# Context projections in blocks of three token tiles, keys in two arrays, keys of two head pairs loaded at once

## The chip, the cores and the metric

The kernel runs on one core of one Trainium2 chip. The metric is the device time of one execution in microseconds (us). Each of the core's engines works through its own list of instructions: TensorE (PE) for products and transpositions, VectorE (DVE), ScalarE (ACT) and GpSimd (POOL) for the rest, and SyncE (SP), which here only issues DMAs and waits. They are kept in step by semaphores. A DMA is carried out by up to 16 DMA engines of the core.

## What is computed

Four layers on x of 16 x 256 x 512, each added to x after a layer norm: a cross attention, a feed-forward layer with quantized weights, a second attention with a mask, and a feed-forward layer with LoRA experts. Only the first is touched. Cut to it:

```python
def _L0_xattn_ref(x, context, Wq, Wk, Wv, Wk_ip, Wv_ip, Wo, bo):   # 16 heads of 64
    ctx_txt = context[:, :77, :]                # 77 of the 256 context rows of a sample
    ctx_img = context[:, 77:, :]                # the other 179
    q = (x @ Wq)
    out = _attend(q, ctx_txt @ Wk, ctx_txt @ Wv)            # softmax(q k / 8) v for each head
    out_ip = _attend(q, ctx_img @ Wk_ip, ctx_img @ Wv_ip)
    return (out + out_ip) @ Wo + bo
x = x + _L0_xattn_ref(_layernorm(x), ctx_1024, ...)
```

All is float32. A product is made of three, with each operand split into a high and a low part (`product`, L189 to L195: high x high, high x low, low x high).

## The kernel before

**Two stages.** `cross_attention` calls `project_context` and then `attend_pairs`. The first makes keys and values of all 16 samples and writes them to DRAM (`k_d`, keys with a row for each of 1024 head dimensions and a column for each of 4096 context tokens; `v_d`, values with a row for each token). It also normalizes x, turns it and writes it (`xn_d`), and splits and turns the gate weights of the next layer (`wg_d`). The second reads all of that back, a pair of heads at a time.

**Blocks.** The text rows and the image rows of the samples have different weights, so `context_blocks` makes blocks of one kind: four of text, each the 77 rows of four samples (308 rows), then eight of image, each the 179 rows of two samples (358 rows). A block is cut into tiles of 128 rows. Where the last tile has fewer, it is loaded from `skip` rows further up, so that it still has 128; the repeated rows are not stored. Both kinds of block have three tiles.

**Jobs.** `jobs_of_block` gives eight key jobs (128 of the 1024 head dimensions for all rows of the block, 4 x 3 products with as many columns as the block has rows) and two value jobs for each tile (128 rows by 512 dimensions, 4 x 3 products with 512 columns). That is 14 jobs in a block, 168 in all. Job j uses the PSUM bank j % 6; ACT copies the result of even jobs to one of six stage slots, DVE of odd jobs (`job_out_of`, L528 and L479), and SP stores the slot (L421). A copy waits until the slot's store of six jobs before has landed (`stored`), and PE waits for the bank's copy of six jobs before (`job_out`).

**What is interleaved.** `turns` is a table of when PE transposes a tile: the next block's context tiles behind the jobs 1, 2 and 3 of a block, four tiles of x behind the jobs 5, 7, 9 and 11 of each image block, and gate weights in between. SP has one list: at job j it loads weight pieces, context rows (`load`, L363, one DMA for each run of rows of one sample within a tile), x rows (`load_x`, L368) and gate weights, then stores the turned tiles and the job's slot. A wait in this list holds up all that stands behind it. There is one buffer for context rows and one for x rows; a load waits until the last tile of the block before has been turned.

**The attention.** 128 steps, one for each sample and pair of heads. SP loads the keys of the pair five steps ahead (`load_k`, L680) into one of four buffers `kr`, in two DMAs of 64 rows, one for each head's half; ACT and POOL split them three and two steps ahead (`keys_high`, L922; `keys_low`, L762). Every second step SP loads values, and in every step it waits for the queries that DVE has finished and stacks them with four DMAs (L695). ACT must see a stack landed before it overwrites its source two steps on (`queries_high`, L953).

Of the kernel before, what the change touches and what calls it, by code (L numbers as in the profile page):

```python
# [16 lines left out]
F32 = mybir.dt.float32  # L17
# [6 lines left out]
P = 128  # L24
B, S, D = 16, 256, 512
TOK = B * S
CT = 512
NCH = TOK // CT
# [5 lines left out]
HEADS, DH = 16, 64  # L34
INNER = HEADS * DH
TEXT = 77
# [159 lines left out]


IMG = S - TEXT
TB, IB = 4, 2


class Rows:
# [16 lines left out]


def context_blocks():
    blocks = []
    for g in range(B // TB):
        blocks.append(Rows("text", g * TB, TB * TEXT, [((g * TB + i) * S, TEXT) for i in range(TB)]))
    for g in range(B // IB):
        blocks.append(Rows("img", g * IB, IB * IMG, [((g * IB + i) * S + TEXT, IMG) for i in range(IB)]))
    return blocks


# [4 lines left out]

def cross_attention(nc, a, x_in, ctx_in, x1, xt_d, wg_d, wq, first_x, big, scal, ident, neghalf):
    xn_d = nc.dram_tensor("xn_parts", (B, P, 2, KD, S), F32R).ap()
    k_d = nc.dram_tensor("k_rows", (INNER, TOK), F32).ap()
    v_d = nc.dram_tensor("v_rows", (TOK, INNER), F32).ap()
    with Phase(nc, "xo", leaf=False) as top:
        wo = top.sb("Wo", [P, 2, NPAIR * D], F32R)  # L240
        project_context(nc, a, x_in, ctx_in, xn_d, k_d, v_d, wg_d, wq, wo, ident, neghalf)
        attend_pairs(nc, a, x_in, xn_d, k_d, v_d, x1, xt_d, wq, wo, first_x, big, scal, ident, neghalf)


def project_context(nc, a, x_in, ctx_in, xn_d, k_d, v_d, wg_d, first, second, ident, neghalf):


    blocks = context_blocks()
    NBLK, NTX = len(blocks), B // TB
    jobs = [(c, job) for c, block in enumerate(blocks) for job in jobs_of_block(block)]  # L250
    first_job = [next(i for i, (c, _) in enumerate(jobs) if c == b) for b in range(NBLK)] + [len(jobs)]
    NJ = len(jobs)
# [30 lines left out]
    with Phase(nc, "pr") as ph:  # L283
        w = [first, second, ph.sb("w2", [P, 2, KD * INNER], F32R), ph.sb("w3", [P, 2, KD * INNER], F32R)]
        raw = ph.sb("raw", [P, NRAW, INNER])
        rows = ph.sb("rows", [P, MOST, D])
# [4 lines left out]
        NQ = D // QB  # L291
# [22 lines left out]
        def stores(j):  # L314

            c, job = jobs[j]
            block = blocks[c]
            slot = stage[:, j % NST]
            if job[0] == "k":
                each = TEXT if block.kind == "text" else IMG  # L320
                off, nb = (0 if block.kind == "text" else TEXT), block.n // each
                cols = slice(block.first * S, (block.first + nb) * S)
                return [(k_d[job[1] * P:(job[1] + 1) * P, cols].rearrange("p (b n) -> p b n", n=S)[:, :, off:off + each],
                         slot[:, 0:block.n].rearrange("p (b n) -> p b n", n=each))]
            lo, count, skip = block.tiles[job[1]]
            cols = slice(job[2] * CT, (job[2] + 1) * CT)
            return [(v_d[row:row + length, cols], slot[skip + at:skip + at + length, :]) for at, row, length in block.pieces(lo, count)]
# [28 lines left out]
        with nc.Block() as block_:  # L356
            @block_.sync
            def _(sp):
# [43 lines left out]
                for j in range(NJ):  # L402
                    c = jobs[j][0]
                    for at in range(0 if j == 0 else j + 2, j + 3):
                        for i in piece_at.get(at, []):
                            load_piece(i)
                    if c + 2 < NBLK and j == first_job[c] + len(blocks[c + 1].tiles):
                        load(c + 2)
                    if j == first_job[NTX - 1]:
                        load_x(0)  # L410
                    for i in range(KF):
                        if j == first_job[WFIRST + i // WPER - 1] + WAT[i % WPER] + 1:
                            load_gate(i)
                    if c >= NTX and c + 1 < NBLK and j == first_job[c] + 12:
                        load_x(c - NTX + 1)
                    for n, kind, _, _ in turns_at.get(j - 1, []):
                        if kind != "c":
                            store_aside(n)
                    sp.wait_ge(job_out[j % 2], j // 2 + 1)
                    for dst, src in stores(j):  # L420
                        sp.dma_start(dst, src).then_inc(stored[j % NST], 16)  # L421
# [168 lines left out]
def attend_pairs(nc, a, x_in, xn_d, k_d, v_d, x1, xt_d, wq, wo, first_x, big, scal, ident, neghalf):  # L590
# [13 lines left out]
    with Phase(nc, "at") as ph:  # L604
# [35 lines left out]
            ph.sem(n) for n in ("row_max", "all_max", "settled", "spacer_d", "spacer_p", "spacer_a"))  # L640
        cleared, bo_ready, bo_high, bo_low = (ph.sem(n) for n in ("cleared", "bo_ready", "bo_high", "bo_low"))
        x_ready, v_ready = ([ph.sem(f"{n}{i}") for i in range(2)] for n in ("x_ready", "v_ready"))
        q_ready, k_ready = [ph.sem(f"q_ready{i}") for i in range(NQ)], [ph.sem(f"k_ready{i}") for i in range(NKR)]
        res_ready, stored = ([ph.sem(f"{n}{i}") for i in range(NY)] for n in ("res_ready", "stored"))
        s_full, max_done, exp_done, sum_done, rec_done, norm_done, v_high, v_placed, k_high, k_low = (
            ph.sem(n) for n in ("s_full", "max_done", "exp_done", "sum_done", "rec_done", "norm_done", "v_high", "v_placed", "k_high", "k_low"))
# [18 lines left out]
        with nc.Block() as block:  # L665
            @block.sync
            def _(sp):
# [5 lines left out]

                def load_k(n):
                    b, h = n // NPAIR, 2 * (n % NPAIR)
                    cols = slice(b * S, (b + 1) * S)
                    if n >= NKR:
                        sp.wait_ge(k_low, n - NKR + 1)
                    for rows in (0, 64):
                        sp.dma_start(kr[rows:rows + 64, n % NKR], k_d[h * DH:(h + 2) * DH, cols].rearrange("(h r) n -> r h n", r=DH)  # L680
                                     ).then_inc(k_ready[n % NKR], 16)

                def load_v(g):
                    b, p = g // (NPAIR // 2), g % (NPAIR // 2)
# [28 lines left out]
                load_x(0)  # L713
                load_k(0)
                load_v(0)
                for n in range(1, LEAD_K - LEAD_Q + 1):
                    load_k(n)
                sp.wait_ge(cleared, 1)
                for row in (0, 32):
                    sp.dma_start(xn[row:row + 1, :], a["L0_xattn_bo"].rearrange("(o n) -> o n", o=1)).then_inc(bo_ready, 16)  # L720
                load_x(1)
                for s in range(FIRST, LAST + 2):
                    if FIRST < s and s + LEAD_K < N:
                        load_k(s + LEAD_K)
                    if 0 < s + 1 < N and s % 2:
                        load_v((s + 1) // 2)
                    if 0 <= s < N and s % NPAIR == 0:
                        load_res(s // NPAIR)
                    if s >= 0 and (s + 10) % NPAIR == 0 and 2 <= (s + 10) // NPAIR < B:
                        load_x((s + 10) // NPAIR)  # L730
                    if s + LEAD_Q < N:
                        stack_q(s + LEAD_Q)
                    done = s - LAG_O - NPAIR - 2
                    if done >= 0 and done % NPAIR == 0:
                        store(done // NPAIR)
                    if out_tile(s - 4):
                        store_turned(*out_tile(s - 4))
                    if s == N:
                        sp.wait_ge(q_full, N)
                        for i in range(2):  # L740
                            sp.wait_ge(xt_stored[i], 16 * NB * NTE // 2)
                        sp.dma_start(wq[:, 0, 0:KD * CT].bitcast(F32), xt_d[0]).then_inc(first_x, 16)
# [147 lines left out]
            def _(act):  # L890
# [25 lines left out]
                    ins.then_inc(exp_done, 1)  # L916

                def keys_high(n):
                    act.wait_ge(k_ready[n % NKR], 32 * (n // NKR + 1))
                    if n >= NK:  # L920
                        act.wait_ge(s_full, n - NK + 1)
                    act.activation(ks[:, n % NK, :, 0, :], kr[:, n % NKR], ACT.Copy).then_inc(k_high, 1)  # L922
# [1974 lines left out]
```

## Time and profile before

| | us |
|---|---|
| median of three runs (3362.14 to 3363.12) | 3362.61 |
| the profiled execution | 3366.48 |
| its span, first to last instruction | 3364.4 |
| PE busy in the span | 3144.0 (93%) |
| DVE, ACT, POOL busy | 1965.9, 1665.2, 792.3 |
| context projection, from the first to the last product of it | 22 to 445 |
| first attention | 456 to about 1240 |

The profile has one execution. A line of a timeline gives the start, the length, the engine (SPq and the like are an engine's issuing of DMAs), the line of the code, the operation, output<-input, and how many instructions are merged; in brackets the idle time before it and what ended it. Matmuls are pipelined, so the pace of a row of products is read from their starts and not from their lengths. The share of the DMA engines is a mean over 16.

### The profile page before, as it was taken

The page shows a single profiled execution, that of the slowest core. Times are in us where ns is not written, and L with a number is a line of the kernel's source. Part 1 is how long each engine was busy: PE and PEld are TensorE (multiplying, and loading weights), DVE is VectorE, ACT ScalarE, POOL GpSimd, SP SyncE. Part 2 cuts the span into 40 slices and gives each one's busy share as a digit, 9 for nine tenths or more (in the row PEclk, how much of TensorE's full clock was granted, in tenths as well). Part 3 has the DMA queues.
Part 4 walks back from the last instruction along what each step waited for, and adds up shares of the span by engine and source line. Part 5 has one row for each costly group of instructions (what it writes and reads, how often), then busy time and mean ns, then how long its engine had stood idle before and what let it go on. Part 6 is the DMA issues. An engine that isn't in the chain of part 4 may idle for free. (4 is left out here: it accounts for less than half of the span.)

```text
span 3364.4 us, 51211 instructions
## 1 busy us (share of the span) xinstructions
PE 3144.0 (93%) x16792; PEld 2687.5 (80%) x16792; DVE 1965.9 (58%) x3425; ACT 1665.2 (49%) x3210; POOL 792.3 (24%) x882
## 2 busy tenths in 40 slices
PE   7999979999999979999996798996979999999998
PEld 6988969999999957887874576885857888888886
DVE  3245549999999965557888995554843222222211
ACT  3132249999999953336676786564722111111110
POOL 0000038888888830000000200003700000000000
PEclk9999989999999999999998898998989999999999
DMA  6487755555555545556666676444831110001000
GB/s 187 120 250 228 228 171 165 172 177 173 171 167 173 158 154 195 180 172 204 225 217 220 215 261 224 156 162 158 265 116 60 38 38 27 24 26 38 32 26 13
DMA packets 370165, 503.46 MB, mean 150 GB/s; under 512 B 58940, under 2 KB 237420, under 8 KB 366032
## 3 DMA queue, kind: packets, MB, share of 16 engines
q1 hardware_dynamic: 356458, 473.37, 45.0%
q0 software_dynamic: 4768, 18.88, 1.6%
q10 hardware_dynamic: 8720, 8.41, 0.7%
q8 instruction: 124, 2.03, 0.2%
q14 instruction: 95, 0.78, 0.1%
HBM read 292.86 MB, written 174.11 MB: 139 GB/s over the span
## 5 line engine op out<-in xcount | busy, mean ns | idle before, releaser
L2625 DVE SCALAR_TENSOR_TENSOR lf_hT<-lf_hb,lf_hT 128x512 fp32r<-128x512 f32 x128 | 88.5, 691 | 571.0 <-ACT lf_hT L2701 571.0
L2701 ACT ACTIVATE lf_hT<-lf_hb 128x512 fp32r<-128x512 f32 x128 | 76.6, 598 | 669.1 <-PE lf_py L195 639.6
L775 POOL TENSOR_TENSOR at_prob<-at_prob,at_rec 128x308 f32<-128x308 f32 (+1 forms) x256 | 261.3, 1043 | 85.5 <-DVE at_rec L815 85.2
L915 ACT ACTIVATE at_prob<-at_sc,at_nm 128x77 f32<-128x77 f32 (+1 forms) x1024 | 277.8, 386 | 6.9 <-DVE at_nm L802 4.5
L193 PE MATMUL lf_hb<-lf_xT,lf_w 128*128 128x512 f32 x512 | 204.8, 400 | 1.3 <-DVE lf_hT L2625 1.3
L195 PE MATMUL lf_hb<-lf_xT,lf_w 128*128 128x512 f32 x512 | 203.7, 398 | 0.0
L195 PE MATMUL lf_py<-lf_w,lf_hT 128*128 128x512 f32 x512 | 203.7, 398 | 0.0
L193 PE MATMUL lf_py<-lf_w,lf_hT 128*128 128x512 f32 x512 | 203.4, 397 | 0.0
L194 PE MATMUL lf_hb<-lf_xT,lf_w 128*128 128x512 f32 x512 | 203.3, 397 | 0.0
L194 PE MATMUL lf_py<-lf_w,lf_hT 128*128 128x512 f32 x512 | 203.2, 397 | 0.0
L808 DVE TENSOR_REDUCE at_sums<-at_prob 128x4 f32<-128x308 f32 (+1 forms) x256 | 166.1, 676 | 17.3 <-ACT at_prob L915 17.1
L2554 POOL TENSOR_SCALAR lf_var<-lf_mv 128x1 f32<-128x1 f32 x32 | 7.3, 229 | 716.4 <-DVE lf_mv L2577 716.4
L193 PE MATMUL at_qb<-at_xT,xo_Wq 128*128 128x256 f32 x512 | 150.0, 293 | 23.5 <-DVE at_qst L832 12.3
L762 POOL TENSOR_TENSOR at_ks<-at_kr,at_ks 128x512 fp32r<-128x512 f32 x128 | 165.4, 1292 | 13.0 <-ACT at_ks L922 13.0
L193 PE MATMUL dn_py<-qf_wd,dn_om 128*128 128x512 f32 x384 | 150.7, 393 | 15.9 <-DVE dn_om L1969 15.9
L802 DVE TENSOR_REDUCE at_nm<-at_sc 128x4 f32<-128x308 f32 (+1 forms) x256 | 159.6, 665 | 5.9 <-PE at_sc L991 5.9
L193 PE MATMUL pg_bank<-qu_xs,qg_wg 128*128 128x512 f32 x384 | 153.6, 400 | 8.7 <-DMA qg_wg<-gate_parts 8.7
L819 DVE TENSOR_TENSOR at_pT<-at_tp,at_pT 128x1024 fp32r<-128x1024 f32 x128 | 156.4, 1222 | 3.4 <-ACT at_pT L928 0.3
L193 PE MATMUL pu_bank<-qu_xs,qu_wu 128*128 128x512 f32 x384 | 150.6, 392 | 7.6 <-SPq L1298 5.7
L1014 PE MATMUL at_sc<-at_pT,at_vs 128*128 128x256 f32 x1024 | 153.1, 292 | 1.4 <-issue 1.4
L194 PE MATMUL pg_bank<-qu_xs,qg_wg 128*128 128x512 f32 x384 | 151.1, 394 | 0.0
L195 PE MATMUL pg_bank<-qu_xs,qg_wg 128*128 128x512 f32 x384 | 150.6, 392 | 0.0
(338 smaller groups left out, 9218.0 us busy)
## 6 DMA issues: line engine op xcount, KB each, us to landing
at_kr<-k_rows SPq DMA_DIRECT2D x256, 128.0 KB, 3.0
at_qs<-at_qst SPq DMA_DIRECT2D x512, 64.0 KB, 2.0
raw_gate<-pg_stage SPq DMA_DIRECT2D x96, 256.0 KB, 2.0
pu_rg<-raw_gate SPq DMA_DIRECT2D x96, 256.0 KB, 3.3
raw_up<-pu_stage SPq DMA_DIRECT2D x96, 256.0 KB, 2.4
om_raw<-raw_up SPq DMA_DIRECT2D x48, 512.0 KB, 4.5
dn_raw<-raw_up SPq DMA_DIRECT2D x48, 512.0 KB, 3.8
xn_parts<-pr_xturned SPq DMA_DIRECT2D x32, 512.0 KB, 5.0
```

The lines of the kernel that those rows point to most:

```text
L193: pe.matmul(out, lh, rh, start=start, stop=False, **kw)
L194: pe.matmul(out, lh, rl, start=False, stop=False, **kw)
L195: return pe.matmul(out, ll, rh, start=False, stop=stop, **kw)
L762: pool.tensor_tensor(ks[:, n % NK, :, 1, :], kr[:, n % NKR], ks[:, n % NK, :, 0, :].bitcast(F32), ALU.subtract).then_inc(k_low, 1)
L775: ins = pool.tensor_tensor(prob[:, i, :, lo:hi], prob[:, i, :, lo:hi], rec[:, z, g, :].unsqueeze(2).broadcast_to([P, 2 * NTE, hi - lo]), A ...
L802: ins = dve.tensor_reduce(nm[:, n % 2, g, :], sc[n % 2][:, :, lo:hi], AX_X, ALU.max, negate=True)
L808: dve.tensor_reduce(sums[:, z, g, :], prob[:, i, :, SEG[g][0]:SEG[g][1]], AX_X, ALU.add).then_inc(sum_done, 1)
L819: dve.tensor_tensor(pT[:, n % 2, 1], tp[:], pT[:, n % 2, 0].bitcast(F32), ALU.subtract).then_inc(pt_done, 1)
L915: ins = act.activation(prob[:, i, m, lo:hi], sc[n % 2][:, m, lo:hi], ACT.Exp, bias=nm[:, n % 2, g, m:m + 1])
L1014: ins = pe.matmul(attended(s)[:, h, :], vs[:, n % NVP, k, h, :, :].rearrange("p a d -> p (a d)"), pT[:, n % 2, part, k, h * S:(h + 1) * S] ...
L2625: dve.scalar_tensor_tensor(hT[:, i, 1, :], hb[i][:], 0.0, hT[:, i, 0, :].bitcast(F32), ALU.max, ALU.subtract).then_inc(h_done, 1)
L2701: act.activation(hT[:, m % 2, 0, :], hb[m % 2][:], ACT.Relu).then_inc(h_hi, 1)
```

## The change

- Blocks are cut from all rows of a kind, without regard to samples: text 256, 384, 384, 208 rows and image 176 and seven times 384. So there are 2, 3, 3, 2 tiles of text and 2 and seven times 3 of image, 33 in place of 36; jobs become 162. A tile's rows may come from two or three samples, cut at any row.
- Text keys and image keys go to an array each, without gaps between samples. A key job's store is one run for each row.
- `load_k` loads two head pairs at once, every second step: four DMAs, for each kind and each half, into two buffers. It waits for the split of one pair more (`n - NKR + 2`), and `keys_high` waits for all four.
- `load_x` of the next x tiles stays 12 jobs behind a block's first job; for the image block of 176 rows, which has 12 jobs, that is the next block's first.

```diff
-TB, IB = 4, 2
+TEXT_BLOCKS = (2 * P, 3 * P, 3 * P, B * TEXT - 8 * P)
+IMG_BLOCKS = (B * IMG - 21 * P,) + 7 * (3 * P,)
 def context_blocks():
     blocks = []
-    for g in range(B // TB):
-        blocks.append(Rows("text", g * TB, TB * TEXT, [((g * TB + i) * S, TEXT) for i in range(TB)]))
-    for g in range(B // IB):
-        blocks.append(Rows("img", g * IB, IB * IMG, [((g * IB + i) * S + TEXT, IMG) for i in range(IB)]))
+    for kind, off, length, sizes in (("text", 0, TEXT, TEXT_BLOCKS), ("img", TEXT, IMG, IMG_BLOCKS)):
+        every = Rows(kind, 0, B * length, [(b * S + off, length) for b in range(B)])
+        lo = 0
+        for n in sizes:
+            blocks.append(Rows(kind, lo, n, [(row, count) for _, row, count in every.pieces(lo, n)]))
+            lo += n
+        assert lo == every.n
     return blocks
-    k_d = nc.dram_tensor("k_rows", (INNER, TOK), F32).ap()
+    k_d = {kind: nc.dram_tensor(f"k_rows_{kind}", (INNER, B * n), F32).ap() for kind, n in (("text", TEXT), ("img", IMG))}
             if job[0] == "k":
-                each = TEXT if block.kind == "text" else IMG
-                off, nb = (0 if block.kind == "text" else TEXT), block.n // each
-                cols = slice(block.first * S, (block.first + nb) * S)
-                return [(k_d[job[1] * P:(job[1] + 1) * P, cols].rearrange("p (b n) -> p b n", n=S)[:, :, off:off + each],
-                         slot[:, 0:block.n].rearrange("p (b n) -> p b n", n=each))]
+                return [(k_d[block.kind][job[1] * P:(job[1] + 1) * P, block.first:block.first + block.n], slot[:, 0:block.n])]
-                    if c >= NTX and c + 1 < NBLK and j == first_job[c] + 12:
-                        load_x(c - NTX + 1)
+                    for i in range(NCH - 1):
+                        if j == first_job[NTX + i] + 12:
+                            load_x(i + 1)
                 def load_k(n):
                     b, h = n // NPAIR, 2 * (n % NPAIR)
-                    cols = slice(b * S, (b + 1) * S)
                     if n >= NKR:
-                        sp.wait_ge(k_low, n - NKR + 1)
-                    for rows in (0, 64):
-                        sp.dma_start(kr[rows:rows + 64, n % NKR], k_d[h * DH:(h + 2) * DH, cols].rearrange("(h r) n -> r h n", r=DH)
-                                     ).then_inc(k_ready[n % NKR], 16)
+                        sp.wait_ge(k_low, n - NKR + 2)
+                    for kind, lo, count in (("text", 0, TEXT), ("img", TEXT, IMG)):
+                        keys = k_d[kind][h * DH:(h + 4) * DH, b * count:(b + 1) * count].rearrange("(h r) n -> r h n", r=DH)
+                        for rows in (0, 64):
+                            sp.dma_start(kr[rows:rows + 64, n % NKR:n % NKR + 2, :, lo:lo + count].rearrange("r m h n -> r (m h) n"), keys
+                                         ).then_inc(k_ready[n // 2 % 2], 16)
-                    if FIRST < s and s + LEAD_K < N:
+                    if s + LEAD_K >= NKR and s + LEAD_K < N and (s + LEAD_K) % 2 == 0:
                         load_k(s + LEAD_K)
-                    act.wait_ge(k_ready[n % NKR], 32 * (n // NKR + 1))
+                    act.wait_ge(k_ready[n // 2 % 2], 64 * (n // NKR + 1))
```

How the DMAs stand on SP's queue, at three places. First the start: `pr_rows` are context rows, `pr_raw` pieces of weights, a shape is rows x columns. Before:

```order
L363 DMA pr_rows<-in_ctx_dram 77x512
L363 DMA pr_rows<-in_ctx_dram 25x512
L363 DMA pr_rows<-in_ctx_dram 51x512
L363 DMA pr_rows<-in_ctx_dram 77x512
L379 DMA pr_raw<-in_L_xattn_Wk_dram 128x1024 x4
L363 DMA pr_rows<-in_ctx_dram 77x512
L363 DMA pr_rows<-in_ctx_dram 51x512
```

After:

```order
L364 DMA pr_rows<-in_ctx_dram 77x512
L364 DMA pr_rows<-in_ctx_dram 25x512
L380 DMA pr_raw<-in_L_xattn_Wk_dram 128x1024 x4
L364 DMA pr_rows<-in_ctx_dram 52x512
L364 DMA pr_rows<-in_ctx_dram 76x512
L364 DMA pr_rows<-in_ctx_dram 1x512
```

Two row loads fewer stand ahead of the first weights, and the second block's rows come in other pieces.

Second, the value stores (`v_rows`) at the end of an image block, with the x rows (`pr_xrows`), the turned x (`xn_parts`) and the gate weights between them. Before, in every image block:

```order
L421 DMA v_rows<-pr_stage 51x512
L421 DMA v_rows<-pr_stage 77x512
L368 DMA pr_xrows<-in_x_dram 128x4x512
L395 DMA xn_parts<-pr_xturned 1024x1x128
L421 DMA v_rows<-pr_stage 102x512
L385 DMA pr_raw<-in_L_ffn_w_gate_dram 128x512
L392 DMA gate_parts<-pr_xturned 128x1024
L421 DMA v_rows<-pr_stage 102x512
L421 DMA k_rows<-pr_stage 128x2x179 x3
```

After, in the sixth of the eight image blocks:

```order
L423 DMA v_rows<-pr_stage 128x512 x2
L369 DMA pr_xrows<-in_x_dram 128x4x512
L396 DMA xn_parts<-pr_xturned 1024x1x128
L423 DMA v_rows<-pr_stage 1x512
L423 DMA v_rows<-pr_stage 127x512
L386 DMA pr_raw<-in_L_ffn_w_gate_dram 128x512
L393 DMA gate_parts<-pr_xturned 128x1024
L423 DMA v_rows<-pr_stage 1x512
L423 DMA v_rows<-pr_stage 127x512
L423 DMA k_rows_img<-pr_stage 128x384 x6
```

The pieces of 51, 77 and 102 rows, the same in every image block, have become others, which differ from block to block; here the last tile is one row of a sample and 127 of the next.

Third, the attention: `at_kr` are the keys, `at_vr` the values, `at_qs` the stacked queries, four DMAs a step. Before:

```order
L680 DMA at_kr<-k_rows 64x2x256 x2
L695 DMA at_qs<-at_qst 64x256 x4
L680 DMA at_kr<-k_rows 64x2x256 x2
L687 DMA at_vr<-v_rows 128x2x256
L695 DMA at_qs<-at_qst 64x256 x4
```

After:

```order
L698 DMA at_qs<-at_qst 64x256 x8
L683 DMA at_kr<-k_rows_text 64x4x77 x2
L683 DMA at_kr<-k_rows_img 64x4x179 x2
L690 DMA at_vr<-v_rows 128x2x256
L698 DMA at_qs<-at_qst 64x256 x8
```

The keys have left every second step, and four of their DMAs stand in the others ahead of the values.

## Rows read from the trace of the kernel before

**Rows 1.** Stretches: busy us of each engine, granted clock, DMA share, GB/s

```profile
31.50:156.10 124.60, 124.59 (x696) 112.04 (x697) 35.87 (x51) 31.19 (x51) 0.00 (x0) 0.99 0.60 154
156.10:191.55 35.45, 35.45 (x197) 32.10 (x196) 18.69 (x31) 12.47 (x19) 1.28 (x2) 1.00 0.78 233
228.28:264.64 36.36, 36.36 (x205) 32.93 (x204) 19.30 (x38) 8.79 (x16) 1.26 (x2) 1.00 0.73 223
470.80:1230.00 759.20, 740.46 (x5485) 693.23 (x5484) 701.91 (x1337) 695.77 (x1848) 612.05 (x668) 1.00 0.55 162
```

**Rows 2.** Waits of PE between 60 and 446 us, the whole answer

```profile
PE pr_tp L555 <- DVE pr_xrows L449: 1.1, 1, 1.1
```

**Rows 3.** Timeline of PE in an image block: key products, a turn, value products

```profile
245.71 0.33 PE L193 MATMUL pr_bank<-pr_turned,pr_w 128*128 128x358 f32 x1
...
246.20 0.60 PE L555 MATMUL pr_tp<-ident,pr_xrows 128*128 128x128 f32 x4
246.55 0.48 PE L193 MATMUL pr_bank<-pr_w,pr_turned 128*128 128x512 f32 x1
246.87 0.39 PE L194 MATMUL pr_bank<-pr_w,pr_turned 128*128 128x512 f32 x1
247.10 0.40 PE L195 MATMUL pr_bank<-pr_w,pr_turned 128*128 128x512 f32 x1
...
251.97 0.39 PE L195 MATMUL pr_bank<-pr_w,pr_turned 128*128 128x512 f32 x1
```

**Rows 4.** Timeline of the start: SP's loads, the third tile's turn, PE's wait

```profile
10.54 1.97 PE L555 MATMUL pr_tp<-ident,pr_rows 128*128 128x128 f32 x8 [10.54 <-DMA pr_rows<-in_ctx_dram]
...
20.38 1.12 PE L555 MATMUL pr_tp<-ident,pr_rows 128*128 128x128 f32 x4 [7.87 <-DVE pr_turned L470]
21.53 2.38 SPq L363 DMA_DIRECT2D pr_rows<-in_ctx_dram  x7
...
22.34 0.63 PE L193 MATMUL pr_bank<-pr_turned,xo_Wq 128*128 128x308 f32 x1 [0.84 <-DVE pr_turned L470]
...
31.51 0.66 PE L555 MATMUL pr_tp<-ident,pr_rows 128*128 128x128 f32 x4 [4.02 <-DMA pr_rows<-in_ctx_dram]
```

**Rows 5.** DMA packets of 151.9 to 154.2, 146.9 to 149.6 us; stretch inside the second

```profile
DMA packets 157, 0.26 MB, mean 114 GB/s; under 512 B 29, under 2 KB 29, under 8 KB 157
...
DMA packets 143, 0.26 MB, mean 98 GB/s; under 512 B 14, under 2 KB 14, under 8 KB 143
...
148.50:148.90 0.40, 0.40 (x3) 0.34 (x2) 0.00 (x0) 0.06 (x1) 0.00 (x0) 1.00 0.20 77
```

**Rows 6.** DMA packets of four image blocks, 228.28 to 373.8 us

```profile
DMA packets 34555, 33.48 MB, mean 230 GB/s; under 512 B 1545, under 2 KB 26122, under 8 KB 34545
```

**Rows 7.** Attention, timelines of SP, POOL, ACT; page's DMA rows; a key store's stretch

```profile
668.06 1.28 SPq L680 DMA_DIRECT2D at_kr<-k_rows  x2
...
671.32 2.41 SPq L695 DMA_DIRECT2D at_qs<-at_qst  x4
...
668.00 1.28 POOL L762 TENSOR_TENSOR at_ks<-at_kr,at_ks 128x512 fp32r<-128x512 f32 x1
...
679.46 0.43 ACT L953 ACTIVATE at_qst<-at_qb 128x256 fp32r<-128x256 f32 x1
679.73 0.69 ACT L922 ACTIVATE at_ks<-at_kr 128x512 fp32r<-128x512 f32 x1
...
at_kr<-k_rows SPq DMA_DIRECT2D x256, 128.0 KB, 3.0
at_qs<-at_qst SPq DMA_DIRECT2D x512, 64.0 KB, 2.0
...
141.00:141.80 0.80, 0.80 (x5) 0.63 (x5) 0.00 (x0) 0.00 (x0) 0.00 (x0) 1.00 0.91 193
```

## What was expected of the change

> **What bounds the kernel now.** I read the stretches first. From 31.5 to 445 us, the projection of the context, TensorE (PE) is busy without a break [rows 1], and its one wait after 60 us is 1.1 us [rows 2]. The granted clock there is 1.00, the 2.4 GHz level. So PE work taken out of this stage is time taken out of the kernel, as long as nothing else comes late. From 471 to 1230 us, the attention that reads the keys, PE is busy 740.5 of 759.2 us [rows 1]: bound by PE as well, and the change takes no PE work from it. The stages behind it are untouched. In the first 31.5 us PE waits for rows and weights [rows 4].
>
> What else is close to its limit in the projection? ACT and DVE are busy for half of an image block or less; the DMA engines are busy for 0.73 to 0.78 of it as a mean over 16 [rows 1]. Whether that mean is evenly spread decides this case, so I looked at single transfers.
>
> **PE work.** (a) Value products: a block of 308 or 358 rows takes three tiles, the last one partly repeated. 36 tiles become 33, and a tile is two jobs of 12 products with 512 columns, so 72 fall away. From 246.87 to 251.97 us 22 of them start, 0.232 us each [rows 3]: 72 x 0.232 = -16.7 us. (b) Turns of context tiles: three fewer. From the turn's start to the second product behind it 0.67 us pass, where one product takes 0.23 [rows 3]: 3 x 0.44 = -1.3 us. (c) Key products: 96 jobs of 12 both times, and the same columns in sum. Three with 358 columns take 0.49 us, 0.163 each, and 512 take 0.232 [rows 3]: 0.00045 us a column and 0.003 fixed. Same count, same columns: 0, bounds -1 and +3 (blocks of 176 and 208 columns may meet a floor of the weight loads). Sum: -18.0 us, all on PE's path.
>
> **The start.** Block 0 has two tiles, so its first product no longer waits for the third tile, which is turned only after DVE has taken the first (20.38 to 22.34 us) [rows 4]: -2 us. Loads for block 1, issued at 21.53 because they wait for the last turn [rows 4], can go right behind the weights, since both turns are over by 12.5; the 4.0 us that PE waits at 31.5 may shrink. Against that, DVE turns block 1 behind the next weight piece, and block 2's rows land unevenly (below). I take -2 in all, bounds -6 and +3. One more edge: the x rows of the second image block are now loaded at its own first job instead of four jobs ahead; they must land some 10 us later. A wait of 0 to 4 us on PE, in my middle below.
>
> **DMA: the term that decides.** A store of 26, 77 and 25 rows leaves 29 packets below 512 bytes, and one of 77 and 51 leaves 14 [rows 5]. These are the engines' completion marks: 13 + 11 + 5 and 11 + 3. Each is the largest divisor up to 16 of the number of rows. Between 148.5 and 148.9 us only the store of 51 rows runs: 0.20 of 16 engines, 77 GB/s [rows 5]. So three engines carry 17 rows each, at 25.6 GB/s or 0.080 us a row, while 13 idle. (By the page "DMA: Bandwidth & Descriptors" of the Trainium skill, section "Why a DMA increments its semaphore by 16 and not by 1", a transfer runs on the largest k up to 16 that divides its slowest dimension, on the lowest-numbered engines, and 127 partitions on one. The marks agree with k; no row before has a prime above 16, and none names the engines. By that page of the Trainium skill the sum below holds; were the engines taken in turn, it would be rival A.)
>
> The old cuts fell on 128, 77, 51, 102 rows: 16, 11, 3, 6 engines. The new cuts walk through the samples, and pieces of 79, 53, 101, 127 and 103 rows appear, which have no divisor: by the pattern one engine takes them all, 127 rows 10.2 us, for the load and for both value stores. I count the rows of the first engine, assuming that the dealing always begins there. Before, an image block gives it 40 for its load and 98 for its stores: 138, where an even deal of 384 + 716 gives 69. Its excess is 69 x 0.080 = 5.5 us. After, for the image blocks I0 (176 rows) to I6, the block's stores with the loads of the block two further on: 128, 274, 334, 299, 383, 345, 278 (I6 has none to load). Sum 2041; an even deal would give 454; the excess is 1587 x 0.080 = 127 us.
>
> To this comes the even part of a block. Low: 230 GB/s [rows 6] over 36.4 us is 8.4 MB, at 16 x 25.6 GB/s 20.4 us. High: the measured share, 0.75 x 36.4 = 27.3 us [rows 1]. Before, the first engine thus had 26 to 33 us in 36.4: it fits, as the trace shows. After, for I0 to I6 (6.7 blocks by their even work): 127 + 137 to 127 + 183 = 264 to 310 us. PE has 6 x 37.5 (the 36.4 and 26 more columns in 96 products) + 24 = 249. The first engine is short by 15 to 61 us. I take 24 us for the even part, nearer to the low end, because an engine that lags works alone and packets stretch only when all 16 run: 127 + 161 = 288, short by 39.
>
> Two things come to this. Six stage slots and six banks let PE run some 12 jobs ahead of the stores, and I7 is light (102 rows of stores): -10 to -20 us of the lag is made up there. Against that, x rows and weights queue behind the lag and stop DVE, and a PE that stops drops to 1.2 GHz, as the second stretch's 0.99 shows after the wait of 4.0 us; both +10 to +20 us. I let them cancel: **+40 us**, bounds 0 and +80. The stores wait for slots, so ACT and DVE stand at their copies out of the banks (L528, L479), and PE at the job that needs the bank.
>
> **Keys in attention.** Instead of two DMAs for each head pair in every step, four in every second step, each again with 64 rows outermost: an even deal. SP now waits for the split of a pair one step later (`k_low` n - 2). At 668.06 SP issues its load, and that split ends at 669.28 [rows 7], so SP stands 1.2 us, in half of the cases. Behind it on SP's queue are the loads of values and residuals and the stacking of queries. That begins at 671.32; with 1.2 us of waiting and two more issues of 0.64 it begins some 1.1 us late, and lands by 677 instead of 675.7 (issue 2.4 and landing 2.0 us). ACT next needs it at 679.46 [rows 7]. The keys, issued by 669.3 and 3.0 us on their way, landed at 672.3 and may now land at 676; ACT takes them at 679.73. Both stay covered by the steps ahead: 0. If that cover were gone, 62 late loads at 1.1 us would cost 68 us. Packets of 1024 bytes become 308 and 716. A store of 308-byte pieces moves 193 GB/s at a share of 0.91 [rows 7], 13 GB/s an engine, half the pace of whole rows. 32768 of them at 0.023 us over 16 engines are 47 us in a stretch of 759 where the engines idle 0.45: hidden. (The same page of the Trainium skill, "Specifications", wants 512 bytes for line rate and speaks of a read-modify-write below; the row agrees on half the pace. Against the pace of whole rows it is 22 us more on each engine, hidden here by the same idle share, so the sum is one by both.) Key stores become one run of up to 1536 bytes instead of 308 or 716: a little for the engines, inside the range.
>
> **Sum.** -18 - 2 + 40 + 0 = +20 us. The profiled execution took 3366.5 us, span 3364.4 and 2.1 around it, 3.9 more than the median of the runs; from it 3386.5, from the median 3362.6 **3382 us**.
>
> **Rivals.** (A) The change gives what PE saves: the engines rotate from DMA to DMA, or the run-ahead swallows the lag. 3362.6 - 20 = 3343 us. For it: PE hardly waited before although the first engine had up to 33 of 36.4 us. Against it: the count more than doubles in five blocks. 0.17. (B) The lag is at its low end, 15 to 25 us, and eats the gain: 3358 to 3368, no change. 0.17. (C) My forecast, slower, the one engine behind; it decides from a lag above 27 us: 0.45. (D) The same mechanism at its high end, with late rows and half clock on top: +60 to +80, 3403 to 3423 us. 0.16. (E) Slower in attention: the stacked queries miss ACT's turn once SP's delay is above 3.5 us, 68 us: 3411 with PE's gain. 0.03. (F) The change does not do what it says: no, the 72 products are gone from the program; 0.02 for a gain that falls to something unnamed, at either end.
>
> **How the numbers follow.** Runs agree within 0.03%; 0.2%, 6.7 us, is what I count as told from no change. Faster is A and half of F: 0.18. Same is B: 0.17. Slower is C, D, E and the rest: 0.65. The range must leave out 2 in 10: it begins at 3346, leaving out the better half of A, and ends at 3420. C's own range is 3370 to 3400.
>
> **What will show it.** Value products fall from 864 to 792 at 0.23 us. If C is right, PE shows waits between 160 and 470 us, first in I2 and longest in I4 to I6, on copies out of the banks that themselves wait for stores of `v_rows`, or on `pr_rows` and `pr_xrows`; the DMA share falls below 0.7 while one engine works; the projection ends near 465 instead of 445. If A is right it ends at 426. In attention the steps keep their 5.6 to 6.0 us. It would be wrong if primes are dealt over several engines (more than one completion mark for a piece of 127 rows).

## The result and the profile after

The changed kernel took 3393.95 us (median of four runs, 3392.24 to 3395.94), the kernel before 3362.38 beside it (3359.48 to 3363.12). The ratio is 1.0094, 95% interval 1.0082 to 1.0106: slower by 31.6 us. The profiled span is 3393.3 us, 28.9 more than before.

Where it was lost shows in two long stretches, set out as in [rows 1]: length, busy us of PE, its weight loads, DVE, ACT and POOL with their instructions in brackets, granted clock, DMA share, GB/s. The first runs from the first to the last product of the context projection, the second from the first to the last product that writes attention scores. Before:

```profile
22.34:445.34 423.00, 417.92 (x2324) 377.29 (x2324) 185.41 (x336) 105.70 (x181) 10.15 (x16) 1.00 0.70 205
470.79:1234.78 763.99, 741.48 (x5489) 693.84 (x5488) 704.32 (x1343) 696.58 (x1849) 612.59 (x669) 1.00 0.55 161
```

After, the same two, and behind them the eight image blocks I0 to I7, each from its first key product to that of the next:

```profile
19.86:477.92 458.06, 412.74 (x2244) 373.15 (x2244) 182.34 (x331) 102.22 (x176) 10.92 (x16) 0.96 0.58 186
501.40:1267.15 765.75, 743.44 (x5489) 695.87 (x5488) 704.40 (x1343) 696.65 (x1849) 612.66 (x669) 0.99 0.57 160
...
143.77:168.92 25.15, 24.77 (x174) 22.55 (x172) 12.62 (x25) 8.30 (x15) 1.28 (x2) 1.00 0.58 171
168.92:216.72 47.80, 39.36 (x200) 35.33 (x199) 21.29 (x35) 13.20 (x21) 2.05 (x2) 0.93 0.78 243
216.72:253.94 37.22, 37.22 (x206) 33.87 (x205) 19.52 (x38) 8.93 (x16) 1.26 (x2) 1.00 0.68 222
253.94:297.50 43.56, 39.16 (x205) 34.91 (x204) 19.23 (x38) 8.76 (x16) 1.26 (x2) 0.96 0.57 191
297.50:338.58 41.08, 37.52 (x205) 33.70 (x204) 19.24 (x38) 8.77 (x16) 1.26 (x2) 1.00 0.65 210
338.58:386.74 48.16, 39.82 (x205) 35.65 (x204) 19.51 (x38) 8.77 (x16) 1.26 (x2) 0.89 0.61 196
386.74:432.37 45.63, 38.77 (x206) 34.92 (x204) 19.52 (x38) 8.87 (x16) 1.27 (x2) 0.93 0.44 148
432.37:477.92 45.55, 38.05 (x193) 34.17 (x191) 17.73 (x35) 7.19 (x13) 1.26 (x2) 0.93 0.59 196
```

The projection is 35.1 us longer, though it holds 80 recorded PE instructions fewer. PE idles in it for 458.06 - 412.74 = 45.3 us, where it idled 5.1. An image block took 36.4 us before, PE busy to the end of it at a clock of 1.00 [rows 1]; only I2 is still like that. The blocks from I5 on take 45 to 48 us, at a DMA share of 0.44 to 0.61 instead of 0.73: there the transfers hold up the kernel while the DMA engines look idler in the mean. I1 is another case, 47.8 us at a share of 0.78; the longest of its waits, 5.4 us, is for the x rows that are now loaded at its own first job (2.4 us in the version with even cuts below). The attention differs by 1.8 us in 764.

PE's waits from 20 to 480 us, the whole answer (waiting instruction, what released it, us in total, times, longest), where [rows 2] had one wait of 1.1 us:

```profile
PE pr_tp L557 <- DVE pr_xturned L472: 18.7, 5, 8.3
PE pr_tp L557 <- DVE pr_xrows L451: 13.3, 3, 7.5
PE pr_bank L193 <- DVE pr_turned L472: 9.2, 1, 9.2
PE pr_tp L557 <- DVE pr_turned L472: 8.3, 2, 5.8
PE pr_tp L557 <- DVE pr_raw L1106: 5.1, 2, 3.0
```

The 9.2 is the start. The others all stand at a turn (L557), never at a product. One of them, followed backwards at 405 to 413 us, shows why. First PE, ACT, DVE and SP in the timeline (start, us, engine, line, instruction; in brackets the idle time before it and what ended that):

```profile
405.51 0.34 PE L195 MATMUL pr_bank<-pr_turned,pr_w 128*128 128x384 f32 x1
412.71 0.87 PE L557 MATMUL pr_tp<-ident,pr_xrows 128*128 128x128 f32 x3 [6.86 <-DVE pr_xturned L472]
...
411.94 0.49 ACT L530 ACTIVATE pr_stage<-pr_bank 128x384 f32<-128x384 f32 x1 [10.08 <-DMA k_rows_img<-pr_stage]
412.33 0.59 ACT L522 ACTIVATE pr_xturned<-pr_tp 128x512 fp32r<-128x512 f32 x1
...
411.41 0.56 DVE L481 COPY pr_stage<-pr_bank 128x384 f32<-128x384 f32 x1 [8.97 <-DMA v_rows<-pr_stage]
411.88 0.68 DVE L472 TENSOR_TENSOR pr_xturned<-pr_tp,pr_xturned 128x512 fp32r<-128x512 f32 x1
...
384.99 5.81 SPq L386 DMA_DIRECT2D pr_raw<-in_L_ffn_w_gate_dram  x1
391.16 0.34 SPq L393 DMA_DIRECT2D gate_parts<-pr_xturned  x1
391.56 0.89 SPq L423 DMA_DIRECT2D v_rows<-pr_stage  x2
392.49 12.70 SPq L423 DMA_DIRECT2D k_rows_img<-pr_stage  x4
```

PE stops for 6.9 us because its turn needs a bank that DVE has not emptied. DVE's copy of that turned tile (411.88) stands in its row behind a job's copy (411.41) that had waited 9.0 us for its stage slot, until a store of values had left it; ACT's job copy had waited 10.1 us. And SP does not merely queue transfers: its four issues of `k_rows_img` take 12.7 us, the first alone 10.15. What was under way, from the DMA view of 384 to 393 us (transfers issued, KB each, median us to landing):

```profile
v_rows<-pr_stage SPq DMA_DIRECT2D x2, 254.0 KB
pr_raw<-in_L_ffn_w_gate_dram SPq DMA_DIRECT2D x1, 256.0 KB, 14.8
...
v_rows<-pr_stage SPq DMA_DIRECT2D x2, 2.0 KB
```

And the stretch behind that, PE's stop and the start after it, as stretches:

```profile
394.30:403.30 9.00, 9.00 (x57) 8.90 (x56) 7.31 (x18) 2.10 (x4) 1.27 (x2) 1.00 0.08 31
...
405.85:412.71 6.86, 0.00 (x1) 0.03 (x1) 1.16 (x2) 0.77 (x2) 0.00 (x0) 0.71 0.19 72
409.00:415.30 6.30, 2.59 (x8) 2.24 (x9) 3.00 (x5) 1.58 (x3) 0.00 (x0) 0.50 0.40 129
```

Two value stores of 254 KB, 127 rows of 2 KB, were issued, each with its one row beside it. For 9 us the share is 0.08 of 16 engines, 31 GB/s, little above the 25.6 GB/s of one engine that [rows 5] gave. (The Trainium skill, page "DMA: Bandwidth & Descriptors", section "Why a DMA increments its semaphore by 16 and not by 1", puts 127 partitions on a single engine; this stretch agrees, with the 0.08.) The load of gate weights issued among them, 256 KB, needed 14.8 us to land. Then PE stands, and for 6.3 us from 409.0 on its clock is 0.50, the 1.2 GHz level. I5 has a stop of the same kind of 8.3 us, and I7 one of 7.5 us on x rows.

In attention and on the page, the rows that answer to [rows 7]: the stacked queries land in 2.4 us (2.0 before), the image keys in 3.3 (all keys: 3.0 before); and the count of small packets rose from 58940 to 75336.

```profile
DMA packets 382081, 502.67 MB, mean 148 GB/s; under 512 B 75336, under 2 KB 249720, under 8 KB 377948
...
at_qs<-at_qst SPq DMA_DIRECT2D x512, 64.0 KB, 2.4
...
at_kr<-k_rows_img SPq DMA_DIRECT2D x128, 179.0 KB, 3.3
```

### The profile page after: what moved, and what is told of

Same layout as the page of the kernel before. It is cut to its first block and busy times, and to the rows that moved or that the text cites. A ratio compares the mean times of both kernels' runs of the same rounds, so it can differ in the third digit from the quotient of the medians.

```text
span 3393.3 us, 51040 instructions
## 1 busy us (share of the span) xinstructions
PE 3133.5 (92%) x16708; PEld 2679.2 (79%) x16708; DVE 1958.8 (58%) x3419; ACT 1662.9 (49%) x3204; POOL 792.8 (23%) x882
## 5 line engine op out<-in xcount | busy, mean ns | idle before, releaser
L193 PE MATMUL dn_py<-qf_wd,dn_om 128*128 128x512 f32 x384 | 150.3, 391 | 15.9 <-DVE dn_om L1971 15.9
L193 PE MATMUL pg_bank<-qu_xs,qg_wg 128*128 128x512 f32 x384 | 153.8, 400 | 8.7 <-DMA qg_wg<-gate_parts 8.7
L481 DVE COPY pr_stage<-pr_bank 128x384 f32<-128x384 f32 (+4 forms) x81 | 47.1, 582 | 182.7 <-PE pr_bank L195 128.3
L194 PE MATMUL pg_bank<-qu_xs,qg_wg 128*128 128x512 f32 x384 | 151.1, 393 | 0.0
```

Source lines behind the costliest of these rows:

```text
L193: pe.matmul(out, lh, rh, start=start, stop=False, **kw)
L194: pe.matmul(out, lh, rl, start=False, stop=False, **kw)
```

## The experiments

Four theories were set against each other. **T**: the first DMA engine, to which pieces of odd lengths give most or all of their rows, is the bound of the projection. **L**: late loads or the order of the work. **K**: the new key arrays and paired loads. **Q**: SP, which stands in the issue of a transfer and so holds back all others. In the first four experiments Q is no more than the number of SP's issues; the standing came in with the later ones.

**Both kinds of transfer cut evenly, in the changed kernel.** Every piece of a load of context rows and of a value store becomes a multiple of 16 rows and a rest.

```diff
+def evenly(pieces):
+    out = []
+    for at, row, length in pieces:
+        most = length - length % 16
+        out += [(at, row, most)] if most else []
+        out += [(at + most, row + most, length - most)] if length > most else []
+    return out
...
-   ... for at, row, length in block.pieces(lo, count)]
+   ... for at, row, length in evenly(block.pieces(lo, count))]
...
-   ... for piece in block.pieces(lo - skip, P)] ...
+   ... for piece in evenly(block.pieces(lo - skip, P))] ...
```

> The changed kernel, with each context-row load and value store of n rows cut into its largest multiple of 16 and the rest (53 = 48 + 5), so that no piece without a divisor falls on one DMA engine; some 24 more DMA issues per image block. Theory T (the first DMA engine is the bound): its rows in an image block fall from 230 to 430 to about 75, its lag goes, PE's saving is left: 3362 - 18 - 3 = 3341 us, 3336 to 3350, the projection ends near 425 us. Theory L (the waits come from the x rows loaded later and the short first image block, whatever the dealing): 3380 us or more. Theory Q (SP is the bound, by the number of its issues): slower than the changed kernel, above 3394.

Measured: 3345.28 us (3342.14 to 3347.91), the kernel before 3360.22 in the same comparison, ratio 0.9955 (0.9938 to 0.9971). The 48.7 us come back, and the changed kernel with this edit is faster than both. The projection, from the first to the last product:

```profile
20.48:425.91 405.43, 401.07 (x2244) 365.01 (x2244) 183.00 (x331) 103.59 (x176) 10.95 (x16) 1.00 0.66 212
```

And PE's only waits on x rows, from 50 to 480 us:

```profile
PE pr_tp L567 <- DVE pr_xrows L461: 2.8, 2, 2.4
```

Idle time of PE is 4.4 us again, the clock 1.00, though SP issues more transfers (588 against 373 in the first 480 us, by my count over its records). So Q in its first form falls, and L, which had expected 3380 us or more, with it: the x rows stand at the same place of SP's list as in the change.

**The keys alone.** The blocks of before, with the two key arrays and the paired loads:

```diff
-    k_d = nc.dram_tensor("k_rows", (INNER, TOK), F32).ap()
+    k_d = {kind: nc.dram_tensor(f"k_rows_{kind}", (INNER, B * n), F32).ap() for kind, n in (("text", TEXT), ("img", IMG))}
...
-                    for rows in (0, 64):
-                        sp.dma_start(kr[rows:rows + 64, n % NKR], k_d[h * DH:(h + 2) * DH, cols]...
+                    for kind, lo, count in (("text", 0, TEXT), ("img", TEXT, IMG)):
+                        keys = k_d[kind][h * DH:(h + 4) * DH, b * count:(b + 1) * count]...
+                        for rows in (0, 64):
+                            sp.dma_start(kr[rows:rows + 64, n % NKR:n % NKR + 2, :, lo:lo + count]...
```

> The kernel before with the key part alone: text and image keys in arrays of their own, keys of two head pairs loaded at once every second step, blocks as before. T: the attention stays bound by PE, steps of 5.78 us: 3362 us, within 4. Rival K (the new loads of 308 and 716 bytes and SP's wait reach the path): 10 us or more slower.

Measured: 3360.45 us against 3360.22, ratio 0.9995 (0.9985 to 1.0005). The keys cost or bring nothing beyond this interval, -5 to +2 us: K falls, and what the change costs lies in the blocks.

**The load on one engine, put into the kernel before.** Nothing is changed but the value stores of 128 rows (the first tile of an image block), which are cut into 127 and 1:

```diff
+def one_engine(pieces):
+    out = []
+    for at, row, length in pieces:
+        out += [(at, row, length)] if length != P else [(at, row, P - 1), (at + P - 1, row + P - 1, 1)]
+    return out
...
-   ... for at, row, length in block.pieces(lo, count)]
+   ... for at, row, length in one_engine(block.pieces(lo, count))]
```

> The kernel before with one thing changed: the value stores of an image block's first tile, 128 rows, are cut into 127 and 1 (two DMA issues more per block). T: the first engine's rows in a block rise from 138 to about 376, its time to 20 to 27 + 25 us against 36.4 us of PE, so 8 to 15 us are lost in each of eight blocks, less some 15 that run beside PE: +50 to +105 us, 3412 to 3467. L and Q: 3362 to 3366, since the bytes, the jobs and the order are the same.

Measured: 3479.44 us, ratio 1.0351 (1.0331 to 1.0372): +119 us for stores of the same bytes. L and Q had expected no change; T's mechanism holds, but the time is 12 us above its upper end. The projection as one stretch:

```profile
22.96:545.75 522.79, 440.88 (x2324) 395.47 (x2324) 185.14 (x336) 105.09 (x181) 10.16 (x16) 0.92 0.55 163
```

PE's wait for the first products of attention, which was 11.1 us before:

```profile
PE at_qb L193 <- DMA at_xT<-xn_parts: 26.4, 1, 26.4
```

SP's row of the timeline in an image block:

```profile
234.25 14.81 SPq L429 DMA_DIRECT2D v_rows<-pr_stage  x4
```

And the DMA view of 234 to 250 us in 40 slices (share in tenths, GB/s):

```profile
DMA  9995000000000200000000000000000000000000
GB/s 293 287 293 142 5 0 5 15 26 26 26 26 26 67 26 26 26 26 26 26 26 26 26 26 26 26 26 26 26 26 26 26 26 26 26 26 26 26 26 26
```

26 GB/s for nearly 13 us with one packet after another: one engine at work, 15 idle. Both stores of 127 rows are issued in this time, at 234.25 and 239.16 us, and one of them lasts 10.2 us at this pace; still the rate does not double. That fits two stores on the same engine, and not each on another in turn, though a second store held back whole behind the first would look alike. That a store of 127 rows has one engine shows in the packets between 235.6 and 251.8 us:

```profile
DMA packets 982, 0.80 MB, mean 50 GB/s; under 512 B 2, under 2 KB 794, under 8 KB 981
```

The two below 512 bytes are the completion marks of the first store, one for its 127 rows and one for its single row. More than one mark for 127 rows was to show the prediction wrong; there is one.

The projection grew by 99.8 us, of which 23.0 are PE work at the lower clock (440.88 against 417.92). Another 15.3 come behind it, because the turned x rows (`xn_parts`) that attention begins with stand in the same queue. T's number had neither this tail nor the lower clock.

**Even cuts in the kernel before.** The edit of the first experiment, on the pieces of before:

> The kernel before with its own row pieces cut into multiples of 16 and a rest. T: the first engine was not the bound before (26 to 33 of 36.4 us), so only the drain behind the last product and the start can gain: 3362 us, -5 to +2. Q: +3 us or more from the added issues.

Measured: 3358.11 us, ratio 0.9993 (0.9984 to 1.0003). The kernel before had an excess too (5.5 us a block in the prediction), but it was hidden: its removal brings nothing. So what the even cuts bring in the changed kernel is not a merit of smaller transfers.

**Stores alone, loads alone.** Each half of the first edit in the changed kernel: `evenly` around the pieces of the value stores only, or around those of the loads only.

> The changed kernel with only the value stores cut into a multiple of 16 rows and a rest; the loads of context rows keep their pieces of any length. Theory T, the first DMA engine is a sum of rows, whoever moves them: its rows in image blocks I0 to I6 fall from 2041 to about 1040, which takes 1000 x 0.080 us = 80 us from an engine that was late by 49 us; it is late no more, and the time is 3343 to 3355 us, as with both cut. Theory L, the loads are what hurts, since the PE waits for turned context rows and x rows: their rows are not cut, so most of the 49 us stays, 3375 to 3394 us. Theory Q, SP standing in the issue of a store: the stores are what hurts, 3343 to 3350 us, and SP's issues of over 1.5 us fall from some 126 us to under 30.

> The changed kernel with only the loads of context rows cut into a multiple of 16 rows and a rest; the value stores keep their pieces. Theory T: the first DMA engine's rows in I0 to I6 fall from 2041 to about 1570, 470 x 0.080 us = 38 us of the 49 us by which it was late; some 11 us stay, 3350 to 3372 us. Theory L, the loads are what hurts: all comes back, 3343 to 3350 us. Theory Q, the stores in whose issue SP stands: their rows are not cut, so little comes back, 3378 to 3394 us.

Measured: stores even 3354.07 us (3345.97 to 3356.50), ratio 0.9969 (0.9960 to 0.9979); loads even 3369.93 us (3365.30 to 3374.30), ratio 1.0026 (1.0016 to 1.0036); the kernel before 3362.53 beside them. Both lie in T's range, neither in that of L, nor in that of Q. The table puts the four versions in a row. The rows on the first engine are my count over the loads and value stores of the eight image blocks, with the prediction's rule. The pieces of the text blocks, which the edits cut as well (742 rows on that engine in the change, 270 with both even), are not in it. A median is over the runs of a version, a span is that of its profiled execution.

| version | rows on the first engine | median us | span |
|---|---|---|---|
| both even | 587 | 3345.28 | 3340.4 |
| stores even | 1144 | 3354.07 | 3348.6 |
| loads even | 1701 | 3369.93 | 3367.8 |
| the change | 2258 | 3393.95 | 3393.3 |

By the count, each step adds 557 rows, and by the span each costs more: 8.2, 19.2 and 25.5 us (8.8, 15.9 and 24.0 by the medians), which is 0.015, 0.034 and 0.046 us a row, on the way to the 0.080 us that a row takes. The uneven loads cost 8.2 us where the stores are even and 25.5 where they are not; the uneven stores cost 27.4 and 44.7. So neither is the cause by itself, and each costs more where the other is uneven too. That fits one resource on which both add up; that a piece of 127 rows is on a single DMA engine was seen for the stores, in the experiment above. That it is the same engine for loads and stores rests on this count and on the rate in that experiment; no view tells the 16 engines apart. The projection in the two, stores even and then loads even:

```profile
19.25:433.88 414.63, 403.49 (x2244) 367.13 (x2244) 182.71 (x331) 103.14 (x176) 10.95 (x16) 0.99 0.64 206
```

```profile
20.69:451.62 430.93, 407.07 (x2244) 369.20 (x2244) 182.87 (x331) 103.60 (x176) 10.95 (x16) 0.98 0.62 199
```

**The x rows issued by ACT.** The changed kernel, but with the loads of x rows taken out of SP's row (the lines removed) and put into ACT's, ahead of the job's copy (the lines added):

```diff
-                    for i in range(NCH - 1):
-                        if j == first_job[NTX + i] + 12:
-                            load_x(i + 1)
...
+                    for i in range(NCH - 1):
+                        if j == first_job[NTX + i] + 12:
+                            act.wait_ge(t_full, number["x", i, NT - 1] + 1)
+                            act.dma_start(xrows[:], x_in[(i + 1) * CT:(i + 2) * CT, :]...).then_inc(x_ready, 16)
```

> The changed kernel with one thing moved: the seven loads of x rows for the image blocks I1 to I7 are issued by ACT, at the same place of the row of jobs, and no longer by SP, which stands up to 10.15 us in the issue of a value store or of a key store while the first DMA engine works its queue down. All rows of the first engine stay as they are. Theory T, the first DMA engine alone sets the pace: the x loads have rows on it too and queue there whoever issues them, the PE waits for them or for a bank instead, and the time stays within 5 us of the changed kernel, 3389 to 3397 us. Theory Q, what costs the time is that SP holds back the other transfers behind a store that it can't issue: the PE's waits for x rows, 13.3 us in all, go, and the time falls by 8 to 13 us, 3381 to 3386 us.

Measured: 3386.34 us (3383.82 to 3386.63), 7.6 less than the change; ratio to before 1.0071 (1.0054 to 1.0088). That is between the two expectations, nearer to Q's. PE's waits of 50 to 480 us:

```profile
PE pr_tp L558 <- DVE pr_xturned L469: 17.8, 5, 6.4
PE pr_tp L558 <- DVE pr_turned L469: 8.2, 2, 4.8
PE pr_tp L558 <- DVE pr_xrows L448: 5.2, 3, 3.8
PE pr_tp L558 <- DVE pr_raw L1107: 4.5, 2, 3.0
```

The wait on x rows falls from 13.3 to 5.2 us, by the 8 that the time falls. The waits that follow from full stage slots stay. So SP's standing is a part of the way in which one engine's lag reaches PE, worth about 8 of the 48.7 us through the x rows; T's claim that it makes no difference who issues them does not hold: it had allowed 5 us, and the interval of this ratio overlaps that of the change (1.0082 to 1.0106) only at its end. How much it adds through the gate weights and context rows was not tried.

## Why the prediction was right, point by point

**The verdict and the place** were right: slower, by the one engine behind (its case C), and in the projection; 3382 was forecast with 3346 to 3420, 3393.95 came.

**PE work**, -18.0 us: in the projection without the lag (both even) PE is busy 401.07 us against 417.92, -16.9. Right. Within it, key products did meet a floor: those with 176 columns follow each other every 0.112 us, and so do those with 208 (13 and 17 starts on in the rows below), where 0.00045 us a column and 0.003 would give 0.082 and 0.097. For the 96 products of either block that is +4.3 us together. Those with 384 columns take 0.173 instead of 0.176 by the same formula, which in nine blocks gives 2.4 back.

```profile
144.41 0.27 PE L193 MATMUL pr_bank<-pr_turned,pr_w 128*128 128x176 f32 x1
144.52 0.28 PE L194 MATMUL pr_bank<-pr_turned,pr_w 128*128 128x176 f32 x1
...
145.87 0.28 PE L194 MATMUL pr_bank<-pr_turned,pr_w 128*128 128x176 f32 x1
...
129.03 0.27 PE L193 MATMUL pr_bank<-pr_turned,xo_Wq 128*128 128x208 f32 x1
...
130.93 0.28 PE L195 MATMUL pr_bank<-pr_turned,xo_Wq 128*128 128x208 f32 x1
```

**The start**, -2 us: the first product begins at 19.86 instead of 22.34 us. Right. The late x rows of the second image block, 0 to 4 us: with both cut even, PE's longest wait on x rows is 2.4 us. Right.

**The DMA term**, +40 us (0 to +80), is the one that was mis-sized. Measured on the projection against the version with even cuts: 458.06 - 405.43 = 52.6 us. Of these 41.0 are idle time of PE (45.3 against 4.4) and 11.7 are work at the lower clock (412.74 against 401.07). What did not come out is the cancelling: the prediction let the run-ahead of stage slots and banks make up for half clock and late rows, and the half clock alone is 11.7 us on top of the idle time. That the idle time comes near the lag of 39 is in part luck. No run separates what lag, late rows and run-ahead gave in it. About 4.3 us of it stand in the text blocks (a stop of 5.8 us, 1.5 with even cuts), whose pieces the prediction had not counted, and about 8 came by way of SP's standing (the experiment with ACT), which it had not foreseen.

The way to PE was another one as well. The prediction had PE stop at the job that needs a bank; behind the start no wait of PE stands there. All stand at the turns: for a bank whose copy is on ACT or DVE behind copies that wait for a stage slot, or for x rows and weights that came late (13.3 and 5.1 us). And a stop is paid for once more at the lower clock: behind the one of 6.9 us PE does 2.59 us of work in the stretch at 0.50, of which about 1.3 would have been saved at full clock (an estimate from that row). The 0.99 from which the prediction read the lower clock stands in the first row of [rows 1].

**The projection's sum**: -16.9 of PE work, +40.2 of idle time (45.3 against 5.1 before), +11.7 of half clock are the 35.1 measured, and with the start 2.5 earlier it ends 32.6 later, at 477.92 instead of 445.34; 465 was forecast. Behind it 3.7 us come back. By the ends of the stretches above, 2.0 of them lie between the projection and the first scores (25.5 us before, 23.5 after) and 3.5 behind the attention, in stages that the change does not touch; the attention takes 1.8. No run says why.

**Keys in attention**, 0: ratio 0.9995 in the experiment on them. Right; case E falls.

**Rival A**, 3343 us with the projection ending at 426, is what the changed kernel does once the lag is gone: 3345.28 us and 425.91. Its price was right; its condition, an even deal, had to be made by hand.

**What would show it**: the waits were to come first in I2 and be longest in I4 to I6. They came earlier, in the text blocks (5.8 us) and in I1 (2.4 and 5.4), where the prediction had seen only the image blocks' lag from I2 on, and the longest stand in I5 to I7. That copies would wait for stores of `v_rows`, that PE would wait for x rows (13.3 us), and that the share would fall below 0.7 while one engine works, is what the rows show. The copies' waits for a slot, 60 to 480 us:

```profile
ACT pr_stage L530 <- DMA k_rows_img<-pr_stage: 29.5, 4, 10.1
DVE pr_stage L481 <- DMA v_rows<-pr_stage: 26.5, 4, 10.4
DVE pr_stage L481 <- DMA k_rows_img<-pr_stage: 20.1, 2, 10.2
ACT pr_stage L530 <- DMA v_rows<-pr_stage: 18.9, 4, 10.3
```

The copies thus waited for key stores at least as long, 49.6 us against 45.4. These are cut evenly, but SP issues them behind the uneven ones; the prediction had not named them. No wait in that answer ends on the landing of `pr_rows`, which it had.

## What to carry to other kernels

Before a block size is changed, count the rows that every transfer will have: a length with no divisor from 2 to 16, such as 127, put a whole transfer on one engine here. Such lengths can cost several times what the change saves in PE work (52.6 us against 16.9), even where a mean DMA share of 0.7 seems to leave room. Cutting each piece into a multiple of 16 rows and a rest takes a helper of a few lines; where that DMA engine has time to spare, as in the kernel before, it brings nothing (ratio 0.9993). A wait of PE that follows from it shows up as a wait for another engine's copy, so follow it back to the transfer and read the share of just that stretch: 0.08 there says more than 0.58 over the stage.

## What the runs showed of the hardware

**SP stands in an issue.** Behind a store that one engine works off, SP's next issues take 5.81 us, and 12.7 us for four (rows of 384.99 and 392.49 above). With 127 rows in the kernel before, four take 14.81 us, and the two of a single row, each right behind 127, take 4.58 and 9.61 of it. By my count over SP's records of the first 480 us, issues longer than 1.5 us make 11 us before, 126 us after, and 8 us with both cut evenly. The prediction had counted with transfers that queue, not with an issuing engine that stands.

**Most of what is added to one engine reaches the end.** 1920 more rows on it (by the count 378 instead of 138 in each of eight image blocks) are 154 us of its work, of which the kernel before had time to spare for a part; the kernel became 119 us longer. 23 of these are time that PE's work took longer at the lower clock (0.92 in the mean).

**Small key products have a floor** of about 0.112 us, at 176 columns as at 208, where 384 columns take 0.173.
